# Loading x and the context a second time, features first, instead of transposing them on TensorE

## What is computed

```python
# x (8, 256, 256), context (8, 120, 256), W (256, 256), keys (64, 256, 128), values (64, 128, 256), float32
def attention(query, info, W, b):
    q = query @ W.T + b
    return softmax(q @ info.T, axis=-1) @ info          # per batch
def ffn(x, expert_sel, keys, values):
    sel = sigmoid(x @ expert_sel.T)
    val, idx = top_k(sel, 4)
    gates = zeros((N, 64)); gates[arange(N), idx] = val
    h = einsum('nd,kde->nke', x, keys)
    return einsum('nke,kev->nv', relu(h) * gates[:, :, None], values)
x = x + tanh(g_xattn) * attention(layernorm(x), ctx, W, b)
x = x + tanh(g_ffn) * ffn(layernorm(x), expert_sel, keys, values)
```

## Time and profile before

| | us |
|---|---|
| median of three runs | 255.71 |
| lowest and highest | 253.8, 255.84 |
| span of the profiled execution | 254.5 |

### The profile page before, as it was taken

One profiled execution on the slowest core, in us unless ns is written; L12 is line 12 of the kernel. 1 busy time (PEld: TensorE's weight loads), 2 busy tenths in 40 slices (PEclk: granted clock), 3 DMA queues, 4 the chain that ended last, 5 costly groups with the idle time before them and its releaser, 6 DMA issues.

```text
span 254.5 us, 4511 instructions
## 1 busy us (share of the span) xinstructions
PE 191.2 (75%) x1316; PEld 146.4 (58%) x1316; DVE 132.4 (52%) x496; ACT 109.4 (43%) x307; POOL 139.4 (55%) x156
## 2 busy tenths in 40 slices
PE   7866996976976832207999999999999994009873
PEld 6744764654744521004888888887878771007752
DVE  3657268897688877200122222356666552506584
ACT  2555287867686741000345454454555551000111
POOL 4004254777777777760367777777777777700000
PEclk9995699997999655555899999999999998555999
DMA  6999999999999999993769976676666422169996
GB/s 159 239 290 320 358 336 331 343 376 320 329 316 301 284 298 314 337 312 95 223 202 332 333 202 211 195 237 163 186 210 200 132 78 83 62 222 408 385 417 236
DMA packets 40894, 66.01 MB, mean 259 GB/s; under 512 B 5381, under 2 KB 24603, under 8 KB 40864
## 3 DMA queue, kind: packets, MB, share of 16 engines
q1 hardware_dynamic: 32572, 46.68, 60.3%
q0 software_dynamic: 6624, 16.82, 19.1%
q10 hardware_dynamic: 1668, 2.17, 2.3%
HBM read 38.31 MB, written 28.64 MB: 263 GB/s over the span
## 4 chain that ended last, share of the span: by engine, by line
PE 51%; DMA 12%; DVE 11%; POOL 8%; ACT 7%; issue 7%; POOLq 1%; SPq 1%; DVEq 0%; ACTq 0%
PE bank L735 13%; PE bank L764 11%; DMA keys_sb<-y_rows 10%; POOL x_slots L525 7%; PE bank L729 6%; PE bank L567 4%; PE bank L657 2%; PE bank L770 2%; PE bank L754 2%; DMA x_slots<-rows,pos_i 2%; DVE xs L1107 2%; PE bank L620 1%; PE bank L779 1%; PE bank L663 1%; PE bank L672 1%
## 5 line engine op out<-in xcount | busy, mean ns | idle before, releaser
L535 POOL DMA_INDIRECT y_rows<-rows,by_place x74 | 73.5, 993 | 35.8 <-issue 20.4
L525 POOL DMA_INDIRECT x_slots<-rows,pos_i x64 | 63.0, 984 | 46.3 <-DVE pos_i L1090 23.8
L987 ACT COPY xT<-bank 128x512 f32<-128x512 f32 (+1 forms) x38 | 21.8, 575 | 55.7 <-PE bank L729 54.0
L1235 DVE TENSOR_SCALAR shared<-bank 128x256 f32<-128x256 f32 (+1 forms) x38 | 15.9, 418 | 52.6 <-PE bank L735 42.8
L735 PE MATMUL bank<-xT,keys_sb 128*128 128x128 f32 x256 | 38.2, 290 | 0.4 <-ACT xT L987 0.3
L735 PEld LDWEIGHTS bank<-xT,keys_sb 128*128 128x128 f32 x256 | 32.4, 194 | 8.2 <-ACT xT L987 5.7
L764 PE MATMUL bank<-values_sb,shared 128*128 128x256 f32 x128 | 34.4, 385 | 0.2 <-DVE shared L1235 0.2
L1001 ACT COPY rows<-bank 128x512 f32<-128x512 f32 (+1 forms) x38 | 21.8, 576 | 15.3 <-PE bank L764 11.6
L1310 DVE SCALAR_TENSOR_TENSOR xs<-keys_sb,by_place,xs 128x256 f32<-128x256 f32 x36 | 15.6, 481 | 16.7 <-DMA keys_sb<-y_rows 16.3
L764 PEld LDWEIGHTS bank<-values_sb,shared 128*128 128x128 f32 x128 | 21.4, 190 | 3.8 <-issue 2.1
L729 PE MATMUL bank<-ident,rows 128*128 128x128 f32 x148 | 22.5, 277 | 0.0
(11 more groups left out here) (145 smaller groups left out, 314.5 us busy)
## 6 DMA issues: line engine op xcount, KB each, us to landing
x_slots<-values_sb SPq DMA_DIRECT2D x4, 2056.0 KB
rows<-x_slots SPq DMA_DIRECT2D x64, 128.5 KB, 3.6
keys_sb<-y_rows SPq DMA_DIRECT2D x16, 512.0 KB, 5.8
values_sb<-in_L_ffn_values SPq DMA_DIRECT2D x5, 1024.0 KB, 13.5
xs<-in_x SPq DMA_DIRECT2D x8, 256.0 KB, 8.6
out<-xs ACTq DMA_DIRECT2D x7, 256.0 KB, 6.1
values_sb<-in_L_ffn_values SPq DMA_DIRECT2D x1, 1408.0 KB, 27.4
rows<-x_slots SPq DMA_DIRECT2D x40, 32.1 KB
```

The costliest lines, as they stand in the source:

```text
L525: pool.indirect_dma_start(x_slots, bass.IndirectOffsetOnAxis(ap=pos_i[:, t * K + k:t * K + k + 1].bitcast(U32), axis=0), rows[:, t % RB * ...
L535: pool.indirect_dma_start(y_rows, bass.IndirectOffsetOnAxis(ap=result_at[:, t:t + 1], axis=0), y_sb[:, t % R, :], None, bounds_check=last_ ...
L987: act.copy(xgT[:, 2 * ring + part.start:2 * ring + part.stop, :].rearrange("p u d -> p (u d)"), pT(place_of(part, ring))[:, part.start * D ...
L1235: dve.tensor_scalar(hidT[:, 2 * ring + part.start:2 * ring + part.stop, :].rearrange("p u n -> p (u n)"), pH(place_of(part, ring))[:, part ...
```

## The change

The host lays a second copy of x and of the context with the features on the partitions: `x_turned` (128 x 8 x 512 floats) and `ctx_turned` (128 x 2 x 960 floats). SyncE loads `x_turned` into `xT` by batches, three batches ahead, and `ctx_turned` whole into `ctxT`, which now lies in `values_now` and holds all eight batches. `x_T` and `context_T` are gone from TensorE and ACT, with their semaphores. `pS` alternates between two PSUM banks, and the scores of a tile wait for `own_dot` of the tile two before and for their own block of `x_turned`. SyncE's order of the first loads changes; the last five blocks of `x_turned` are issued behind the five groups of weights, each after a wait for scores. The plain x and context are loaded as before, since the sums, the statistics and the attended sum use them.

```diff
-        ctxT = shared[:, 512:512 + C * PAIR].rearrange("p (c m) -> p c m", c=C)
+        ctxT = values_now[:].rearrange("p n a d -> p (n a d)")[:, 0:C * B * M].rearrange("p (c m) -> p c m", c=C)
...
-        pX, pPT, pO, rank_ps = bank[:, 0, 0:D], bank[0:M, 5, 0:P], bank[:, 6, 0:OS], bank[:, 4, 0:E]
-        pS, pStat = bank[:, 2, 0:MS], bank[0:2, 3, 0:PT * P]
+        pPT, pO, rank_ps = bank[0:M, 5, 0:P], bank[:, 6, 0:OS], bank[:, 4, 0:E]
+        pStat = bank[0:2, 3, 0:PT * P]
+        def pS(t): return bank[:, (2, 0)[t % 2], 0:MS]
...
-        CONTEXT_T = {1: 1, 4: 2, 8: 3}
...
+            def turned_context_in(n, first, last):
+                sp.dma_start(ctxT[:, :, first * M:last * M], ctx_turned[:, :, first * M:last * M]).then_inc(ctxT_in[n], 16)
+
+            def turned_tokens_in(b):
+                after(sp, a_S, TB * (b - AHEAD + 1))
+                at = b % AHEAD * TB
+                sp.dma_start(xT[:, at:at + TB, :].rearrange("p s n -> p (s n)"), x_turned[:, b, :]).then_inc(xT_in[b % AHEAD], 16)
+
+            turned_context_in(0, 0, 2)
+            sp.dma_start(wq_sb, w_q.rearrange("(c p) q -> p c q", p=P)).then_inc(wq_in, 16)
+            tokens_in(0)
+            turned_tokens_in(0)
             context_in(0)
-            tokens_in(0)
-            sp.dma_start(wq_sb, w_q.rearrange("(c p) q -> p c q", p=P)).then_inc(wq_in, 16)
+            turned_tokens_in(1)
             tokens_in(1)
+            turned_context_in(1, 2, B)
+            turned_tokens_in(2)
             for n in range(1, B // 2):
                 context_in(n)
                 tokens_in(2 * n)
...
             for n in range(0, E - LATE, 8):
                 weights(n)
+                turned_tokens_in(n // 8 + AHEAD)
...
         @block.tensor
...
-            def x_T(t):
-                if t % TB == 0:
-                    pe.wait_ge(x_in[t // TB], 16)
-                for c in range(C):
-                    mm = pe.transpose(pX[:, c * P:(c + 1) * P], xs[:, t, c * P:(c + 1) * P], ident[:])
-                mm.then_inc(a_T, 1)
...
-                pe.wait_ge(a_Tc, t + 1)
+                after(pe, b_own, t - 1)
+                if t % TB == 0:
+                    pe.wait_ge(xT_in[b % AHEAD], 16 * (b // AHEAD + 1))
...
-                    pe.matmul(pS, xT[:, t % 2, c * P:(c + 1) * P], m_sb[:, c, b, :], start=c == 0, stop=False,
+                    pe.matmul(pS(t), xT[:, t % (2 * RING), c * P:(c + 1) * P], m_sb[:, c, b, :], start=c == 0, stop=False,
...
         @block.scalar
...
-            def context_T(n):
-                act.wait_ge(c_T, n + 1)
-                after(act, c_B, n + 1 if n else 0)
-                after(act, c_S, n + 1 if n else 0)
-                act.copy(ctxT.rearrange("p c m -> p (c m)"), ctx_ps).then_inc(c_Tc, 1)
...
-            def x_T(t):
-                act.wait_ge(a_T, t + 1)
-                act.copy(xT[:, t % 2, :], pX).then_inc(a_Tc, 1)
```

More of the change, by code:

```diff
@@ L49, in after, with flamingo_block @@
     engine.wait_ge(semaphore, count.value * each)
-def flamingo_block(nc, x, ctx, g_xattn, g_ffn, w_q, b_q, expert_sel, keys, values, out):
+def flamingo_block(nc, x, x_turned, ctx, ctx_turned, g_xattn, g_ffn, w_q, b_q, expert_sel, keys, values, out):
     B, S, D = x.shape
@@ L85, in flamingo_block @@
     PAIR = 2 * M
+    AHEAD = 3
     PT = 2 * TB
@@ L229, in flamingo_block @@
         ctx_in = [sem(f"ctx_in{i}") for i in range(B // 2)]
+        ctxT_in, xT_in = [sem(f"ctxT_in{i}") for i in range(2)], [sem(f"xT_in{i}") for i in range(AHEAD)]
         x_in = [sem(f"x_in{i}") for i in range(B)]
@@ L547, in _, with context_here @@
         def _(pe):
-            def context_T(n):
-                pe.wait_ge(ctx_in[n], 16)
-                after(pe, c_Mc, n + 1 if n else 0)
-                after(pe, c_B, n + 1 if n else 0)
-                for c in range(C):
-                    for b in range(2):
-                        mm = pe.transpose(ctx_ps[:, c * PAIR + b * M:c * PAIR + (b + 1) * M],
-                                          ctx_sb[:, 2 * n + b, c * P:(c + 1) * P], ident[0:M, 0:M])
-                mm.then_inc(c_T, 1)
+            def context_here(n):
+                pe.wait_ge(ctxT_in[min(n // 2, 1)], 16)
             def context_M(n):
                 first, last = units[n]
-                pe.wait_ge(c_Tc, first // 2 + 1)
+                context_here(n)
                 after(pe, c_Mc, n)
@@ L568, in context_M @@
                                        wq_sb[:, c, cq * P:(cq + 1) * P],
-                                       ctxT[:, c, at:at + width], start=c == 0, stop=c == C - 1)
+                                       ctxT[:, c, first * M:last * M], start=c == 0, stop=c == C - 1)
                 mm.then_inc(c_M, 1)
@@ L574, in context_B @@
                 first, last = units[n]
-                pe.wait_ge(c_Tc, first // 2 + 1)
+                context_here(n)
                 after(pe, c_Bc, n)
                 after(pe, c_Sc, n)
-                at, width = first % 2 * M, (last - first) * M
+                width = (last - first) * M
                 for c in range(C):
-                    mm = pe.matmul(pBias[:, 0:width], col_sb[:, c, :], ctxT[:, c, at:at + width],
+                    mm = pe.matmul(pBias[:, 0:width], col_sb[:, c, :], ctxT[:, c, first * M:last * M],
                                    start=c == 0, stop=c == C - 1)
@@ L670, in attended @@
                     pe.wait_ge(c_Sc, unit_of_batch(b) + 1)
+                    pe.wait_ge(ctx_in[b // 2], 16)
                 after(pe, b_u, t)
@@ L963, in _ @@
                     act.wait_ge(a_max, t + 1)
-                    act.activation(probs[:, t % 2, :], pS[:, 0:M], ACT.Exp, bias=neg_max[:, t:t + 1],
+                    act.activation(probs[:, t % 2, :], pS(t)[:, 0:M], ACT.Exp, bias=neg_max[:, t:t + 1],
                                    scale=rstd1[:, t:t + 1], accum_out=row_sum[:, t:t + 1]).then_inc(a_exp, 1)
-                    act.copy(own_dot[:, t % 2, :], pS[:, M:MS]).then_inc(b_own, 1)
-                if live(s + 1):
-                    x_T(s + 1)
+                    act.copy(own_dot[:, t % 2, :], pS(t)[:, M:MS]).then_inc(b_own, 1)
                 if s - 1 in CONTEXT_M:
                     context_M(CONTEXT_M[s - 1])
-                if s - 1 in CONTEXT_T:
-                    context_T(CONTEXT_T[s - 1])
                 if s == 0:
@@ L1337 @@
     out = nc.dram_tensor("out", arrays["in_x"].shape, F32, kind="ExternalOutput").ap()
-    flamingo_block(nc, *args, out)
+    B, S, D = arrays["in_x"].shape
+    M = arrays["in_ctx_1024"].shape[1]
+    C, TB = D // P, S // P
+    arrays["x_turned"] = np.ascontiguousarray(
+        arrays["in_x"].reshape(B, P, TB, C, P).transpose(4, 0, 2, 3, 1)).reshape(P, B, TB * D)
+    arrays["ctx_turned"] = np.ascontiguousarray(
+        arrays["in_ctx_1024"].reshape(B, M, C, P).transpose(3, 2, 0, 1)).reshape(P, C, B * M)
+    turned = [nc.dram_tensor(n, arrays[n].shape, F32, kind="ExternalInput").ap() for n in ("x_turned", "ctx_turned")]
+    flamingo_block(nc, args[0], turned[0], args[1], turned[1], *args[2:], out)
     return run_bass_kernel_spmd(nc, [arrays], core_ids=[0]).results[0]["out"]
```

28 lines of the change are left out of this document (9 added, 19 removed).

## The result

The changed kernel takes 261.22 us (median of four runs, 260.87 to 262.13), the kernel before, run beside it, 255.59 (253.8 to 255.84). The ratio is 1.0225, 95% interval 1.0183 to 1.0266. The profiled execution's span is 259.6 us against 254.5, its mean granted clock 0.834 against 0.859.

The account below looks back on a forecast made before the run. GpSimd's scatters and SyncE's load backlog bound the stage before the first gather; 9.2 us of added traffic puts late keys at 124.9 and first gather at 125.1, +5.1 on 254.5: 259.6, median 260.8. Range 254.0 to 264.0.

Parts of the forecast that it names:

- The place and the total: Before the experts' first gather: it moves from 120.0 to 125.1, +5.1 us; the 134.5 us behind it stay unchanged.
- the prediction's own formula: GpSimd's end in the first stage: the largest, over tiles t, of tile t's scatter start + 5.11 x (16 - t).
- The gaps closed by the turned context: Attention front: without transposes and copies, context_M(2) starts directly after scores(2), 2.1 us less; with ACT's 0.3, -2.4 on R(2).
- R(0): Start of tile 0's scatters on GpSimd: predicted to move to 25.6, ending at 107.4 and binding nothing.
- R(2): Start of tile 2's scatters on GpSimd: predicted 41.16 + 4.1 - 2.4 - 1.0 = 41.9, so GpSimd ends near 113.7.
- The clock: TensorE at context_M(2): closer-packed work may meet the full clock sooner, worth 0 to -1.7 us; taken as -1.0.
- The first loads: Front: x of batches 1 and 2 lands later and stalls VectorE; tile 0's addition at 18.4 instead of 14.34, +4.1 us.
- The traffic: SyncE's queue: 3.08 MB of added loads at 334 GB/s cost 9.2 us; late keys land at 124.9 instead of 115.7.
- SyncE's waits, priced at nothing: SyncE's queue: waits for scores before later turned loads; a halt of 2 or 3 us costs nothing while the ring holds work.
- The forecast's own test: First gather: late keys and gathered transposes near 125 would confirm; a gather 4 us behind the last scatter would refute.
- GpSimd is the bound, and late: Rival, first stage: R(2) at 42.9, gather 124.7, total 260.4; no separate chance, slower by backlog or late front together 0.65.
- the traffic fits in: Rival, DMA engines: the 3.08 MB move at no cost, the gather waits for GpSimd alone, +0.7, 256.4 us; chance 0.20.

Follow-up runs that it names:

- late keys behind: Changed kernel with 2.1 MB of late keys issued behind the first twenty gathers; 310.68, 306.96 and 308.62 us on three slow chips (ratios 1.012, 1.010, 0.997).
- the traffic run: Kernel before plus 3.08 MB of unread x loads behind the five weight groups; 259.1 us, ratio 1.0114; on slow chip a 309.87 us, 0.9933.
- x first: Changed kernel with x of batches 0 to 2 loaded ahead of W or later turned blocks; 306.72, 305.90, 306.33 us on three slow chips (1.000, 0.993, 0.985).

## Why the prediction was right, and where it was right by luck

**The place and the total.** All is lost in front of the first gather, and the first gathered rows came at 125.83, for 125.1 in the sum. The span of 259.6 is the one predicted. The experts and the sum took 133.8 instead of 134.5, which takes back the 0.7. (By the prediction's own formula tile 2 would end at 112.7, not at the 112.9 that it gives; nothing rests on it.)

**The gaps closed by the turned context: right.** `context_M(2)` follows `scores(2)` at once, with 2.1 us of waiting gone. The chain of the changed kernel, against the earlier trace rows:

```profile
28.60 0.71 PE bank L665 x2
29.31 3.50 PE bank L577 x8
```

From tile 0 to tile 2 GpSimd gains 2.5 us by it (44.52 - 27.39 = 17.13 against 19.68), for 2.4 in the sum. The other profiles agree in direction: from R(0) to R(2) it is 18.0 to 19.3 us in the eight of kernels without the transposes, 19.4 to 20.9 in the four with them.

**The clock: wrong.** `context_M(2)` takes 3.50 us, 3.57 before: the same lower level. The -1.0 did not come. Worse, the level fell in a stretch in which it had been full: 0.58 from 8 to 17 us, in and behind a pause of TensorE of 3.61 us. The prediction named that idle time and then took the gain all the same. One warning on reading it: late keys behind on chip b has the same front, and there the granted clock reads 1.00, while the same eight matmuls take the same 2.06 us (window, then PE's timeline).

```profile
14.00:17.00 3.00, 3.00 (x12) 2.38 (x12) 0.84 (x5) 0.74 (x4) 0.00 (x0) 1.00 1.08 249
```
```profile
15.47 2.06 PE L577 MATMUL bank<-values_now,shared 128*128 128x120 f32 x8
```

So the level at which TensorE works is read from the length of its instructions; the granted clock alone can miss it. That the pause is what lowered it was not isolated.

**The first loads: late as predicted, but by another wait, and the term too small.** The step was "the addition falls near 18.4 instead of 14.34", from the landings of batch 1 and 2 alone. Batch 2 landed near 17.4 (17.0 in the sum), and VectorE was free for the addition at 18.6; but the addition came at 20.26 and waited for TensorE, so the wait that the prediction named did not set it. What was left out is batch 0. It stood behind the turned context and W and its statistics began at 9.09 instead of 4.93, so TensorE's first use of the statistics came at 10.95 instead of 8.53 (+2.4), and the way from there to the addition took 9.31 us instead of 5.81 (+3.5) at the lower clock. Sum +5.9. The three profiles of late keys behind, with the same first loads, repeat it: that way takes 9.1 to 9.7 us there. Of the +5.9 a part is the scatter of the executions, since the base of 14.34 itself comes at 13.7 to 15.9; the means of the two groups of four lie 5.3 apart. The prediction said of the turned x that it stands in the shadow of the statistics; of the statistics' own block it said nothing, though its own rate has that block, with 0.77 MB asked for, in by about 8.3. The front term was +4.1 and is +5.9, the clock -1.0 and is 0, the removal -2.4 and is -2.5: R(2) = 44.5 and not 41.9, above the upper bound of 42.9 that the rival had.

**The traffic: the step that fails.** "At 334 GB/s ... that is 9.2 us" takes the rate at a full share for the rate of a full pipe. The experiment with those bytes alone gives 4.2 us at the late keys, of which up to 1.6 were lost before the first added byte. In the changed kernel the late keys landed at 125.5, as the sum had it (124.9), but then at least 5.6 of the 9.8 us have another cause than the bytes. The DMA view of the first 112 us shows it: packets, MB and mean GB/s of the kernel before, the changed one, and the one with the traffic alone.

```profile
DMA packets 20607, 34.78 MB, mean 311 GB/s; under 512 B 1732, under 2 KB 9542, under 8 KB 20598
```
```profile
DMA packets 20327, 34.59 MB, mean 309 GB/s; under 512 B 1815, under 2 KB 9028, under 8 KB 20318
```
```profile
DMA packets 21476, 36.25 MB, mean 324 GB/s; under 512 B 1797, under 2 KB 9863, under 8 KB 21467
```

With 3.08 MB more to move, the changed kernel had moved no more than the one before; the traffic run, 1.66 MB more than the changed one. At 305 GB/s (the rate from 95 to 112) that is 5.4 us, nearly the 5.6. (Some 0.3 of the 1.66 MB are scatters, which start later in the changed kernel.) Besides, the prediction's "no long stretch here goes above it", said of 358 GB/s, holds for the first stage only: the earlier trace rows end with 408, 385 and 417.

**SyncE's waits, priced at nothing: a part of the missing cause.** In SyncE's queue of the changed kernel, a load of turned x stands behind each group of weights:

```profile
43.69 4.03 SPq L402 DMA_DIRECT2D values_sb<-in_L_ffn_values  x1
53.58 0.34 SPq L381 DMA_DIRECT2D xT<-x_turned  x1
...
54.86 3.09 SPq L402 DMA_DIRECT2D values_sb<-in_L_ffn_values  x1
60.81 0.34 SPq L381 DMA_DIRECT2D xT<-x_turned  x1
61.19 22.38 SPq L416 DMA_DIRECT2D x_slots<-values_sb  x4
```

SyncE issues nothing from 47.72 to 53.58 and from 57.95 to 60.81, while it waits for scores, and twice before (30.31 to 34.54, 39.51 to 42.40): 15.8 us in all, and the padding starts at 61.19 instead of 45.46. The prediction allowed "a halt of 2 or 3 us" under a cover of 13 us of work in the ring. One halt is 5.9 long, and at its end the rate does fall; the windows of the changed kernel:

```profile
48.00:52.00 4.00, 4.00 (x25) 2.52 (x25) 3.62 (x15) 2.91 (x11) 3.09 (x4) 1.00 1.06 335
52.00:56.00 4.00, 3.21 (x30) 2.28 (x29) 3.60 (x14) 3.09 (x12) 2.99 (x4) 1.00 1.02 314
56.00:60.00 4.00, 2.51 (x19) 1.61 (x18) 3.84 (x16) 2.81 (x10) 3.17 (x3) 1.00 0.94 280
```

In the same three windows the traffic run moves 381, 365 and 373 GB/s. The difference is 190 GB/s times 4 us, 0.76 MB of the 1.66; 0.53 MB more are lost from 76 to 84 us, during the padding (258 and 299 against 339 and 350), for which no wait of SyncE stands. That a halt of SyncE can empty the pipe is plain on chip a. In late keys behind, SyncE stands from 47.39 to 56.74 and from 61.64 to 72.84 us before the same two blocks, and the windows from 55 to 60 and from 70 to 75 us are

```profile
55.00:60.00 5.00, 2.17 (x12) 1.35 (x13) 2.60 (x11) 2.59 (x9) 1.44 (x3) 0.63 0.46 126
70.00:75.00 5.00, 1.64 (x14) 1.19 (x13) 1.13 (x5) 0.64 (x3) 2.92 (x3) 0.83 0.43 130
```

The traffic run of the same chip, in which SyncE waits for no scores, has shares of 1.06 and 1.05 there. In both kernels the rate falls some 7 us after SyncE's last issue has ended, so the cover was about 7 us, not 13, and the halt of 5.9 us in the changed kernel just reaches it. How much of the 5.6 us the halts make on the chip of the result is open: the share stays below 1 mainly from 54 to 60 us, and much of the difference arises at a full share. A kernel that loads the blocks without these waits would need a larger `xT`, and none was made.

**The forecast's own test.** It said that a gather 4 us behind the last scatter would speak against it. The gather came 4.5 behind. Late keys near 125 spoke for it. Both ends of the stage arrived within half a us: 125.3 by GpSimd's path (123.7 in the sum; the scatter was issued 2.6 us later and landed after 6.0 us, not 7.1) and the late keys at 125.5. Which decides can't be told from this trace. That a gather is held behind the loads ahead of it, on which the forecast rests, no run shows: only here did the first gather have more than half a us of loads in front of it, and its 4.25 us instead of 3.81 may be the full load alone. The runs meant to tell this apart, x first and late keys behind, ran only on chips on which the backlog does not reach the scatters. So the rival "GpSimd is the bound, and late" is as true as the forecast; it had 260.4.

**The rival "the traffic fits in".** Right about the pipe (a full share took 3.08 MB at half the price or less), wrong in the time: with the traffic alone the kernel is 1.1% slower, of which the profile shows 1.9 us as the last scatter's later landing beside it.

So the total was right by luck. The front was 2.6 us too short at R(2), which brought GpSimd's path up to the forecast by itself; and the traffic term, at least twice too large by its own mechanism, was filled up by other delays of the queue, the waits priced at zero among them.

## What to carry to other kernels

Loads that are added to a queue ahead of others cost by whose landing they push back: list for every block behind them who waits for it, the very first block too, and price each by its landing. A full DMA share at a moderate rate is no full pipe, so price added bytes from both sides, and look besides at what the fuller pipe does to the short transfers on the critical chain. Where a wait is put into the issuing engine's queue, count how long it will stand against what the ring holds, and where two ends of a stage coincide, expect little from mending one of them (so the sums here say; no run on a chip like that of the result tested it). And before a difference of 1 or 2 us between two profiles is given to an edit, see whether it is there already ahead of the edit's first effect.

## What the runs showed of the hardware

- At the same DMA share of 1.05 over 50 us, the engines moved 321 GB/s in one kernel and 357 in another.
- With halts of SyncE of 9 and 11 us (late keys behind, chip a) the DMA share fell from over 1 to 0.46 and 0.43 over 5 us; with one of 5.9 us (the changed kernel) to 0.90 over 2 us.
- The same eight matmuls took 2.06 us at a granted clock of 0.50, 1.05 us at one of 1.00 in the kernel before, and in a third profile 2.06 us though the clock reads 1.00.
- The last scatter took 4.09 us to land in a thinning stream of loads and 6.00 and 6.02 in a full one, not the 7.1 of the whole run's median.
- The same kernel took 255.5 us in two sets of runs and 306 to 311 on three other chips, where engines stop up to 5 us in the first stage with a releaser that the profile gives as "remote" or not at all. The cause is not known.
